# Decays over a chunk: four copies by VectorE, or four small products by TensorE and one copy

## What is computed

```python
dt = softplus(dt_raw + dt_bias)
dA = exp(dt * -exp(A_log))
def step(h, inp):                       # over the 512 tokens of a sequence
    x_t, B_t, C_t, dA_t, dt_t = inp
    h = dA_t * h + (dt_t * x_t) outer B_t
    y_t = sum over states of h * C_t
y = y + D * x
g = rmsnorm_by_group(y * silu(z)) * gate_norm_w
out = residual + g @ out_proj_w
```

## Time and profile before

| | |
|---|---|
| Median of 3 runs | 1287.64 us (1285.94 to 1288.23) |
| The profiled execution | 1288.33 us |
| Its span, first to last instruction | 1286.5 us |
| Mean granted clock of TensorE | 0.975 of full speed |
| PE, products / weight loads | 85% / 56% of the span busy |
| DVE, ACT, POOL | 87%, 76%, 69% |
| DMA | 25.44 MB, 20 GB/s over the span |

### The profile page before, as it was taken

The page is one execution under the profiler, slowest core; times in us unless marked ns, Lnnn a source line. Parts: engine busy times, 40 slices in busy tenths (PEclk is TensorE's granted clock), DMA queues, the critical chain, the costliest instruction groups (busy, mean ns, idle before and its releaser), DMA issues.

```text
span 1286.5 us, 29886 instructions
## 1 busy us (share of the span) xinstructions
PE 1097.4 (85%) x8970; PEld 726.5 (56%) x8970; DVE 1121.1 (87%) x1967; ACT 973.6 (76%) x2798; POOL 887.3 (69%) x600
## 2 busy tenths in 40 slices
PE   0524788999899989998999899989999999987786
PEld 0513566666566656665666566656666666653565
DVE  8788899999789988998999889988999989857995
ACT  2556788888688878887888888878888888852453
POOL 6560367878587867786778778776878788894321
PEclk9998899999899999999999999999999999997999
DMA  5500000000000000000000000000000000100301
GB/s 150 181 0 0 10 2 2 1 2 2 28 2 2 2 28 2 2 2 28 2 2 2 28 2 2 2 27 2 2 2 10 10 2 2 34 26 27 107 25 33
DMA packets 28803, 25.44 MB, mean 20 GB/s; under 512 B 12112, under 2 KB 22992, under 8 KB 28368
## 3 DMA queue, kind: packets, MB, share of 16 engines
q1 hardware_dynamic: 24400, 21.18, 5.4%
q10 hardware_dynamic: 4224, 2.10, 0.5%
HBM read 14.88 MB, written 8.39 MB: 18 GB/s over the span
## 4 chain that ended last, share of the span: by engine, by line
PE 39%; DVE 25%; issue 16%; ACT 12%; POOL 4%; ACTq 1%; DMA 1%; DVEq 1%; POOLq 0%; SPq 0%
DVE conv L1077 8%; PE bank L1441 5%; PE bank L1458 5%; ACT xw L760 5%; DVE lm L1066 4%; PE bank L1464 4%; PE bank L1385 4%; ACT conv L768 3%; PE bank L1401 3%; PE bank L1496 3%; PE bank L1387 3%; PE bank L1386 3%; PE bank L1417 2%; PE bank L1473 2%; DVE cdec L1107 2%
## 5 line engine op out<-in xcount | busy, mean ns | idle before, releaser
L1077 DVE SCALAR_TENSOR_TENSOR conv<-bank,cw,conv 128x511 f32<-128x511 f32 (+2 forms) x576 | 410.1, 741 | 32.6 <-ACT conv L768 30.2
L1066 DVE TENSOR_TENSOR_SCAN lm<-bank,ident 128x512 f32<-128x512 f32 x256 | 298.5, 1208 | 63.8 <-PE bank L1401 51.6
L615 POOL TENSOR_TENSOR lm<-lm,cbs 128x1024 f32<-128x1024 f32 x128 | 303.3, 2369 | 57.0 <-ACT xw L760 56.4
L798 ACT ACTIVATE xdt<-bank,dt_all 128x64 f32<-128x64 f32 x1024 | 222.6, 332 | 0.0
L601 POOL TENSOR_TENSOR gated<-gated,gate 128x512 f32<-128x512 f32 x128 | 164.2, 1283 | 68.9 <-DVE gated L1116 61.1
L760 ACT ACTIVATE xw<-xdt,lm 128x64 f32<-128x64 f32 x768 | 196.3, 339 | 11.7 <-issue 11.7
L621 POOL TENSOR_TENSOR ssum<-ssum,sq 128x512 f32<-128x512 f32 x96 | 123.2, 1284 | 90.9 <-ACT sq L812 88.3
L1385 PE MATMUL bank<-xn_hi,w_hi 128*128 (+1 forms) x320 | 153.2, 479 | 27.9 <-DVE conv L1077 26.0
L607 POOL TENSOR_TENSOR gated<-gated,rbs 128x512 f32<-128x512 f32 x128 | 164.9, 1289 | 1.3 <-ACT rbs L861 1.3
L1441 PE MATMUL bank<-gated,w_out 128*128 128x512 f32 x256 | 151.9, 677 | 4.9 <-POOL gated L607 3.1
L1458 PEld LDWEIGHTS bank<-lm,xdt 128*64 128x64 f32 x2048 | 110.7, 138 | 80.2 <-issue 79.5
(11 more groups left out here) (183 smaller groups left out, 1832.9 us busy)
## 6 DMA issues: line engine op xcount, KB each, us to landing
lm<-in_L_attn_in_proj_w SPq DMA_DIRECT2D x1, 2048.0 KB, 9.8
xn_scratch<-chan SPq DMA_DIRECT2D x4, 512.0 KB, 4.8
r_stage<-residual_scratch SPq DMA_DIRECT2D x8, 256.0 KB, 3.2
x_scratch<-r_stage SPq DMA_DIRECT2D x8, 256.0 KB, 2.3
cbs<-x_scratch SPq DMA_DIRECT2D x8, 256.0 KB, 2.9
gated<-x_scratch SPq DMA_DIRECT2D x1, 2048.0 KB, 8.0
out_tokens<-gated ACTq DMA_DIRECT2D x8, 256.0 KB, 2.3
xn_stage<-xn_scratch SPq DMA_DIRECT2D x7, 256.0 KB, 2.9
```

The source lines that it names most:

```text
L615: gp.tensor_tensor(lm[:, mr, :, :], lm[:, mr, :, :], cbs[:, :, :], ALU.mult).then_inc(m_done, 1)
L798: act.activation(xdt[:, r, at:at + HP], misc_of("xt", n)[:, at:at + HP], ACT.Copy, scale=dt_h).then_inc(xdt_done, 1)
L1066: V.tensor_tensor_scan(lm[:, m % R, a, :], bc_bank[(3 * m + a) % 2][:, :], ident4[:, :], 0.0, ALU.mult, ALU.add).then_inc(scanned, 1)
L1077: V.scalar_tensor_tensor(out=conv[:, ci % 4, shift:S], in0=tile_bank(b, n, t)[:, 0:S - shift], scalar=cw[:, q, t, KW - 1 - shift:KW - shif ...
```

## The change

The decays at the chunk ends are no longer copied from the spread bank, slot by slot. In the state stage of slots with m % 4 = 0 (these are slots r = 2) PE multiplies, for each of the unit's four slots, `sel` with the four chunk-end columns of `pr_parts`, 96 rows by 4 columns, into columns 192 to 207 of the same state bank. `s_ready` now comes with the last of these. DVE copies the 16 columns in one instruction behind state step 0 of that slot, between taps(1) and taps(2), and raises `pend_done` once per unit. State steps 1 and 2 wait for it, in addition to `hstep`. The copy per slot goes; the wait for the spread k = 2 moves from it to `decay_c`.

```diff
+PEND_AT = (CH - 1) * NS
...
                     else:
                         after(dve, hstep, 3 * SLOTS, bb, 3 * m + c - 1)
+                        after(dve, pend_done, UNITS, bb, m // R)
                         V.scalar_tensor_tensor(out=hpk[:, m % 2, c, :], in0=hpk[:, m % 2, c - 1, :],
...
                 def chunk_products():
 
+                    bb, m = state
+                    V.tensor_copy(pend[:, :, :].rearrange("p r c -> p (r c)"),
+                                  misc_of("s", n)[:, PEND_AT:PEND_AT + R * CH]).then_inc(pend_done, 1)
+
+                def decay_c():
+
                     bb, m = ssd
                     after(dve, bc_ready, 3 * SLOTS, bb, 3 * m + 2)
-                    V.tensor_copy(pend[:, m % R, :].unsqueeze(2),
-                                  bc_bank[(3 * m + 2) % 2][:, :].rearrange("p (c i) -> p c i", c=CH)[:, :, P - 1:P]).then_inc(pend_done, 1)
-
-                def decay_c():
-
-                    bb, m = ssd
                     if m % R == 0:
...
                 if state is not None and not one_tile:
                     state_step(0)
+                    if state[1] % R == 0:
+                        chunk_products()
...
-                if ssd is not None:
-                    chunk_products()
...
+                    if m % R == 0:
+
+                        ends = pr_parts[:, bass.ds(bb * S, S)].rearrange("k (c i) -> k c i", c=CH)[:, :, P - 1]
+                        for k in range(R):
+                            last = MM(misc_of("s", n)[:, PEND_AT + CH * k:PEND_AT + CH * k + CH], sel[:, m + k, HP:HP + P], ends,
+                                      start=True, stop=True)
                     last.then_inc(s_ready, 1)
```

## The result

The changed kernel takes 1295.53 us in the median of four runs (1294.42 to 1298.04), the kernel before in the same comparison 1286.79 (1283.97 to 1288.23). The ratio is 1.0073, with a 95% interval of 1.0049 to 1.0098: slower by 0.5 to 1.0%. The forecast was 1286.3, within 1283.5 to 1291.5, with "same" the likeliest. Time and sign came out wrong.

The account below looks back on a forecast made before the run. Only DVE's work from r = 1 to `cdec` of r = 3 was on the path, PE setting the rest; −0.04 us a unit over 32 units, −1.3 us from 1287.64, gave 1286.3 us, range 1283.5 to 1291.5.

Parts of the forecast that it names:

- No DMA, queue or loop edge is touched.: Close of the estimate for PE's added products: nothing outside the slots changes, so no cost was entered there.
- a hole of r = 2: PE's loads idle 0.91 us in r = 2 before the z product, 0.74 of it free for the added products.
- Rival 5: PE's four products take 1.52 us and overrun the idle time in r = 2: +9.0 us, 1296.6; chance 0.06.
- forecast 0.20: DVE, r = 1 and r = 2: without the copy, `cdec` starts 0.20 us after the state step, instead of 0.26.
- forecast 0.08: DVE, r = 2: the new copy per unit holds DVE 0.08 us on the path; bounds 0.07 and 0.17.
- the wait stayed under another name: DVE, r = 3: step 2 waits for step 1 anyway, so removing the copy between them gives 0.00 us.
- rivals 1 to 3: DVE, r=3: step held 0.1 us (1288.1, chance 0.15); held 0.2 (1291.3, 0.12); stall not the step's (1284.4, 0.07).
- the sum of −0.04 us a unit: DVE's total per unit: −0.06 in r = 1, −0.06 + 0.08 in r = 2, 0.00 elsewhere.
- the 0.06 us of one slot: DVE's gain from removing the slot's copy, claimed in r = 1 and in r = 2 each.
- not 0.45: PE, r = 2: four added loads with products take 0.45 us a unit, hidden; bounds 0.2 and 1.52.

Follow-up runs that it names:

- e9: The changed kernel with the loop over b written out on all five engines: 1260.96 us, ratio 0.9793 to the kernel before.
- e8: The kernel before with 24 instructions added under PE's first wait, putting its loop at 1727 as in the changed kernel: 1296.24 us, ratio 1.0054.
- e5: The changed kernel with 28 instructions added under PE's first wait, putting its loop at 1755: 1282.67 us, ratio 0.9946.
- e7: The changed kernel with 232 instructions added under PE's first wait, loop at 1959, 49 ahead of a border: 1290.43 us, ratio 1.0009.
- e6: The kernel before with 52 instructions added under PE's first wait, putting its loop at 1755: 1284.76 us, ratio 0.9967.
- e10: The kernel before with the loop over b written out on all engines: 1260.46 us, ratio 0.979.
- e11: The changed kernel with the loop written out on PE alone; other engines keep their branch: 1273.03 us, ratio 0.9885.

## Why the prediction was wrong

**The step that failed** is the last sentence on PE's products: "No DMA, queue or loop edge is touched." The four products were priced as work in a hole of r = 2, and there they fit. Not priced was that they are instructions, 98 in PE's program and 24 of them ahead of its loop. This moved the border of a packet from 49 to 25 instructions behind the loop's start. The packet behind the border comes as late as before, so that PE runs out of instructions earlier and stands longer, five times over: 6.8 us at the edges, where the prediction had nothing. The trace of before had the sign: beside the rows quoted, its waits of DVE and PE hold five "issue" waits each, of up to 2.5 and 3.6 us, and I didn't ask what sets them. None of the five rivals names the mechanism. Rival 5, at 1296.6, came near the time by another one, which the trace excludes: the z product still waits 0.90 us for a tap. The Trainium skill (Runtime: NRT & Kernel Launch, "Instruction fetch mechanics") says that a taken branch outside what an engine holds stalls it for a fetch, and names unrolling as the way out. The runs agree: 3.3 to 4.4 us for a branch, during which a packet comes, and 27 us won by unrolling. The same section of the Trainium skill says that crossing a 16 KB border is mostly hidden. In straight code that holds here (PE has no "issue" wait in the main stretch of e9), behind a branch it doesn't.

Shown is that the place of the loop decides (e8, e5, e7), and that PE's second stop ends a fixed 1.3 to 1.5 us after the second packet has landed. That the border lies at instruction 1752 is inferred: from the 49 and 25 instructions, from the stop's return to the same instruction in e7, and from its going away in e5 and e6.

**DVE, r = 1 and r = 2.** Timeline of the changed kernel, the unit that answers to the earlier trace rows:

```profile
656.75 0.27 DVE L1093 SCALAR_TENSOR_TENSOR hpk<-hpk,pend,bank 128x64 f32<-128x64 f32 x1
656.94 0.68 DVE L1109 TENSOR_TENSOR cdec<-bank,chan 128x512 f32<-128x512 f32 x1
...
658.19 2.33 DVE L1067 TENSOR_TENSOR_SCAN lm<-bank,ident 128x512 f32<-128x512 f32 x2
660.49 1.41 DVE L1078 SCALAR_TENSOR_TENSOR conv<-bank,cw,conv 128x511 f32<-128x511 f32 x2
...
661.95 0.17 DVE L1100 COPY pend<-bank 128x16 f32<-128x16 f32 x1
662.03 1.40 DVE L1078 SCALAR_TENSOR_TENSOR conv<-bank,cw,conv 128x510 f32<-128x510 f32 x2
...
664.84 0.28 DVE L1093 SCALAR_TENSOR_TENSOR hpk<-hpk,pend,bank 128x64 f32<-128x64 f32 x1
665.03 0.69 DVE L1109 TENSOR_TENSOR cdec<-bank,chan 128x512 f32<-128x512 f32 x1
...
670.75 0.59 DVE L1093 SCALAR_TENSOR_TENSOR hpk<-hpk,pend,bank 128x64 f32<-128x64 f32 x2
671.25 0.68 DVE L1109 TENSOR_TENSOR cdec<-bank,chan 128x512 f32<-128x512 f32 x1
```

Step 2 to `cdec` is 0.19 us in both (forecast 0.20), and the new copy holds DVE for 0.08 (forecast 0.08). In r = 3, steps 1 and 2 together take 0.59, thus start 0.31 apart, and 0.30 to 0.32 in every slot r = 3 of the trace: the wait stayed under another name, as forecast, which rules out rivals 1 to 3. Yet the sum of −0.04 us a unit didn't come. From the scans of the second slot r = 2 of a sequence to those of the fourth, two units on and with no branch between, the changed kernel takes 62.29 to 62.34 us and the kernel before 62.26 to 62.36; without the loop 62.34 to 62.36 (e9) and 62.28 to 62.31 (e10), 0.03 us a unit the other way. In r = 2 the taps start 2.30 us behind the scans (658.19, 660.49), before 2.25; most likely they wait for ACT's first tap (L769), which wasn't in the sum. That takes back most of the 0.06 us of one slot, a size too small to count.

**PE, r = 2.** Weight loads of the changed kernel:

```profile
660.40 0.17 PEld L1440 LDWEIGHTS bank<-pr_parts,sel 96*128 96x128 bf16 x4
660.50 0.30 PEld L1449 LDWEIGHTS bank<-gated,w_out 128*128 128x128 f32 x2
...
664.33 0.19 PEld L1387 LDWEIGHTS bank<-xn_hi,w_hi 128*128 128x128 f32 x1 [0.90 <-DVE conv L1078]
...
665.77 0.10 PEld L1403 LDWEIGHTS bank<-da_parts,sel 96*128 96x128 bf16 x1 [0.55 <-DVE cdec L1109]
```

The four take 0.10 us until the next load, not 0.45: a term mis-sized, but hidden either way. Both later waits are still there, 0.90 us (0.91 in the earlier trace rows) and 0.55 (0.61).

## What to carry to other kernels

- Count instructions and not only their time: what is added ahead of a hardware loop shifts the loop against its packets of 256, and here 24 instructions on PE cost 0.5% with nothing else changed (e8). Look for waits that nothing releases ("issue") behind a branch, as many as there are returns to the loop's start, and at how long the branch instruction itself takes.
- Before judging a small change to a kernel with a loop, compare at equal places of the loop, or without one. Here the change reads as +0.7% as it stands, 0.0% without a loop and −0.2% with both loops at 1755; only the first is clear of noise.
- If the loop's few iterations can be written out, do so on all engines: 2.1% here; on PE alone, whose stop is the longest, half of that.

## What the runs showed of the hardware

- A branch back over the 2316 or 2350 instructions of this loop holds PE for 3.3 to 4.4 us, in 55 of 55 cases, and ends 1.3 to 1.5 us after a 16 KB packet of the instruction queue has landed; a branch back over 269 takes 0.25 us, one not taken 0.08. The five long ones cost 30 us at the edges and 27 of 1287 in the time.
- The next packet starts only 0.65 to 1.24 us after the branch has ended. So PE has what is left of the first packet to work on, and where that is 25 or 49 instructions, it stands again, at 25 for longer.
- The stop lets the granted clock fall to the lower level and it stays there for a while: the twelve loads of L1434 take 0.72 us behind a branch and 0.43 in the middle of a sequence. So a longer stop is paid twice: 13.7 us at the lower level with the loop at 1755, 34.1 to 37.5 with it at 1727, none between 330 and 1010 us in e9, e10 and e11, where PE has no branch there.
- An instruction on PE that only waits for a semaphore that has long fired costs 0.109 us when nothing covers it (232 in 25.2 us).
- Open: why edges of one kernel differ by 2 us, and whether the other engines' loops have a better place too; no run tries either.
